# Moving the last weighted sum of the attention heads from the next step's first slot to the end of its own step

## The chip, the core and the metric

The kernel runs on one core of a Trainium2 chip. The metric is the device time of one execution in microseconds (us); the times given are medians of several runs. The core has five engines that run side by side and meet through semaphores: TensorE (PE in the profile, its weight loads PEld), VectorE (DVE), ScalarE (ACT), GpSimd (POOL) and SyncE (SP), which issues most of the DMAs.

## What is computed

One decoder layer over an input `x` of 32 x 256 x 256 (32 sequence positions, 256 tokens, 256 channels) with a context of the same shape:

```python
x = _layernorm(x + _L0_attn_ref(x, lmlg, theta, last_conv_init))      # long convolution: a complex
                                                                      # decay per channel, real part times x
x = _layernorm(x + _L0_xattn_ref(x, ctx, ctx, ...))                   # cross attention, 16 heads of 16
x = _layernorm(x + _L0_ffn_ref(x, scale, centroids, up_w, down_w))    # each token to one of 8 experts
```

Inside the cross attention, per position:

```python
Qp, Kp, Vp = relu(Q @ Wq + bq), relu(K @ Wk + bk), relu(V @ Wv + bv)
probs = softmax(einsum('bqhd,bkhd->bhqk', q, k) / dh ** 0.5)
out = einsum('bhqk,bkhd->bqhd', probs, v).reshape(B, T, C) + Qp       # then a layer norm
```

The change concerns the second `einsum`, the weighted sum of the values, for the last four of the 16 heads.

## The kernel before

The first part treats one sequence position (256 tokens) as one item, and runs a software pipeline over the 32 items. Each engine has its own instruction list, written out by a function `step(t)` that is called for t = -2 to 34. In one step an engine works on several items at once: `cur` = t gets its scores and their maxima, `prv` = t - 1 its transposed scores, exponentials and weighted sums, `n` = t + 1 its projections, `a` = t - 2 the end of its attention, `b` = t - 3 its routing to the experts, and t + 2 and t + 3 the convolution. The step is cut into 16 places, h = 0 to 15, one for each head. An engine executes its list strictly in the order written; a `wait` holds up all that is behind it on the same engine.

TensorE at each even h computes, for heads h and h + 1, the scores of `cur` (line 1004, to the banks `S`) and the transposed scores of `prv` (line 1017, to the banks `T`). The first scores of a step wait for the stacks of queries and keys, which go through DRAM: GpSimd makes the low pieces `q_lo` and `k_lo` (line 770), SyncE writes them out and reads them back. They wait also for VectorE's maxima of the step before, since there are two banks.

VectorE takes the maxima (line 1243). ScalarE takes the exponentials of `T` (line 864) into the ring `probs`, which holds eight heads. `weighted_sum(item, grp)` (lines 970 to 983) multiplies the probabilities of four heads with the values: 16 matmuls whose outputs are 32 columns each (line 980), into half of the bank `O`. It waits for the four exponentials (`exp_ok`) and for `O` to be free (`o_ev`), and signals `pv`. Groups 0, 1 and 2 run at h = 8, 10 and 13 of the item's step as `prv`. Group 3 runs in the next step, at h = 1, when the item has become `a`. ScalarE copies `O` to `oT` by `copy_sums` (line 854): pair 0 at h = 11, pair 1 in the next step at h = 2. At h = 4 and 5 of that step TensorE transposes `oT` (line 1069), and VectorE divides and adds (lines 1359, 1362, 1370).

Around the place left: at h = 0 TensorE transposes `x1` (line 960), at h = 1 the maxima (`neg_flip`, line 967), which ScalarE copies to `nm_row` in `neg_round` (line 832); SyncE's `write_neg` waits for that. At h = 2 and 3 follows the projection of the queries (line 988), at 6 and 7 that of the keys. Around the place entered: at h = 14 TensorE transposes `q32` (line 1130), at h = 15 the context `ct` for the item after next (line 960), and then comes the next step.

VectorE's order at the start of a step is: maxima 0 and 1, `row` of item `b` (line 1258, waits for GpSimd's `rs`, line 729), maxima 2 and 3, the product `u` (line 1266), maxima 4 and 5. GpSimd's product `by_re` (line 694) belongs to the convolution. `slot` (line 1425, at h = 12) is VectorE's last step of the routing, and releases GpSimd's scatter (line 802).

When all items are through, the second part takes 71 tiles of 128 tokens through their experts (lines 371 to 528). It is the same before and after.

Of the kernel before, what the change touches and what calls it, by code (L numbers as in the profile page):

```python
# [81 lines left out]
def build(nc, x, ctx_in, lmlg, theta, last_conv, Wq, bq, Wk, bk, Wv, bv, ln_g, ln_b, ffn_scale, centroids, up_w, down_w, out):  # L82
    stack = ExitStack()
    with stack:
# [145 lines left out]
        def wait(eng, name, item, per=1, j=None):  # L230

            if not item.runtime and item.k >= SEQ:
                item, j = Item(0, SEQ - 1), per
            wait_value(eng, name, item.times(per, per if j is None else j))
# [28 lines left out]
        def active(item):  # L263
            return item.within(0, SEQ)
# [271 lines left out]
        with nc.Block() as block:  # L536
# [276 lines left out]
            def _(act):  # L813
# [14 lines left out]
                def neg_round(item, half, b):  # L828

                    wait(act, "negT", item, 2, half + 1)  # L830
                    wait_value(act, "neg_out", item.times(32, 16 * half))
                    a_.activation(nm_row[:, :], M_ps[b][0:HPC, 0:TOK], ACT.Copy).then_inc(s["neg_ok"], 1)
# [16 lines left out]
                def copy_sums(item, pair):  # L849

                    wait(act, "pv", item, 4, 2 * pair + 2)
                    if pair == 0:
                        wait(act, "x_pe", item - 1, 2)
                    a_.activation(oT[:, 2 * pair:2 * pair + 2, :].rearrange("p g t -> p (g t)"), O_ps[:, :], ACT.Copy).then_inc(s["o_ev"], 1)
# [12 lines left out]
                def step(t):  # L867
                    prv, n, a, b = t - 1, t + 1, t - 2, t - 3
                    for h in range(H):
                        if h % 2 == 0:  # L870
                            exponentials(prv, h)
                            exponentials(prv, h + 1)
                        if h == 0:
                            if active(n):
                                wait(act, "x1T_pe", n)
                                wait(act, "q_pe", n - 1, 2)
                                a_.activation(x1T[:, :, :].rearrange("p o t -> p (o t)"), M_ps[0][:, :], ACT.Copy).then_inc(s["x1T_ok"], 1)  # L877
                        if h == 14 and active(n):
                            wait(act, "qn_pe", n)
                            wait(act, "oq_ok", n - 4, 2)  # L880
                            a_.activation(qn[:, n.mod(4)].rearrange("p c d -> p (c d)"), M_ps[2][:, :], ACT.Copy).then_inc(s["qn_ok"], 1)
                        if h == 15 and active(n + 1):
                            wait(act, "ctT_pe", n + 1)
                            wait(act, "v_pe", n, 2)
                            a_.activation(ctT[:, :, :].rearrange("p o t -> p (o t)"), M_ps[0][:, :], ACT.Copy).then_inc(s["ctT_ok"], 1)
                        if h == 1 and active(prv):
                            neg_round(prv, 1, 2)
                        if h == 9 and active(t):
                            neg_round(t, 0, 0)
                        if h == 2 and active(a):  # L890
                            copy_sums(a, 1)
                        if h == 3:
                            if active(n):

                                wait(act, "q_pe", n, 2)
                                wait(act, "qn_pe", n - 1)
                                wait_ring(act, q_out[(n - 1).mod(2)], n - 1, 2, 32)
                                for dst in (q_hi, q32):
                                    for c in range(NCH):
                                        a_.activation(dst[:, c], M_ps[0][:, c * TOK:(c + 1) * TOK], ACT.Relu,  # L900
                                                      bias=bq_sb[:, c:c + 1]).then_inc(s["q_ok"], 1)
                        if h == 7 and active(n):
                            wait(act, "k_pe", n, 2)
                            wait(act, "k_cut", n - 1)
                            wait_ring(act, k_out[(n - 1).mod(2)], n - 1, 2, 32)
                            for dst in (k_hi, k32):
                                for c in range(NCH):
                                    a_.activation(dst[:, c], M_ps[1][:, c * TOK:(c + 1) * TOK], ACT.Relu,
                                                  bias=bk_sb[:, c:c + 1]).then_inc(s["k_ok"], 1)
                        if h == 3 and active(b):  # L910
                            wait(act, "xnT_pe", b)
                            wait(act, "dist_pe", b - 1)
                            a_.activation(xnT[:, :, :].rearrange("p o t -> p (o t)"), M_ps[2][:, :], ACT.Copy).then_inc(s["xnT_ok"], 1)
                        if h == 13 and active(n):
                            wait(act, "v_pe", n, 2)
                            wait(act, "pv", n - 4, 4)
                            a_.activation(v_aug[:, n.mod(4), :, 0:H * VW].rearrange("p k (h w) -> p k h w", w=VW)[:, :, :, 0:DH],
                                          M_ps[1][:, :].rearrange("p (k h w) -> p k h w", k=NTC, w=DH), ACT.Relu).then_inc(s["v_ok"], 1)
                        if h == 4 and active(b):

                            wait(act, "xw_ok", b)
                            wait(act, "rms", b, 4)
                            wait(act, "offset", b - 1)
                            for c in range(NTC):
                                if c:
                                    wait(act, "nx_ok", b, 2, 1)
                                a_.activation(junk[:, :], xw[:, c], ACT.Square, scale=row[:, b.mod(2), c, C:C + 1],
                                              accum_out=nx[:, c:c + 1]).then_inc(s["nx_ok"], 1)
                        if h == 11 and active(prv):
                            copy_sums(prv, 0)  # L930
                        for e in HI_AT.get((t.k, h), ()):
                            upper(e)
# [5 lines left out]
            def _(pe):  # L938
# [17 lines left out]
                def flip(dst, src):  # L956

                    for oc in range(NCH):
                        for tc in range(NTC):
                            last = t_.transpose(dst[:, oc * TOK + tc * P:oc * TOK + (tc + 1) * P], src[:, tc, oc * P:(oc + 1) * P], ident[:, :])  # L960
                    return last
# [8 lines left out]
                def weighted_sum(item, grp):  # L970

                    wait(pe, "exp_ok", item, H, 4 * grp + 4)
                    if grp == 0:
                        wait(pe, "v_ok", item)

                    wait_value(pe, "o_ev", item.times(2, grp // 2))
                    for kc in range(NTC):
                        for j in range(4):
                            h = 4 * grp + j
                            last = t_.matmul(O_ps[32 * j:32 * j + 32, (grp % 2) * TOK:(grp % 2 + 1) * TOK],  # L980
                                             v_aug[:, item.mod(4), kc, h * VW:h * VW + 32], probs[:, h % 8, kc, :],
                                             start=(kc == 0), stop=(kc == NTC - 1))
                    last.then_inc(s["pv"], 1)
# [37 lines left out]
                def step(t):  # L1021
                    cur, prv, n, a, b = t, t - 1, t + 1, t - 2, t - 3
                    for h in range(H):
# [8 lines left out]
                        if h == 1:  # L1032
                            if active(prv):
                                wait(pe, "qn_ok", t)
                                neg_flip(prv, 1, 2)
                            if active(a):
                                weighted_sum(a, 3)
                        if h == 2 and n.k == 0:
                            pe.wait_ge(s["params"], PARAMS * 16)
                            pe.wait_ge(s["setup_pool"], 12)  # L1040
# [94 lines left out]
                        if h == 15 and active(n + 1):  # L1135
                            nn = n + 1
                            wait_ring(pe, ctx_in_s[nn.mod(2)], nn, 2, 16)
                            wait(pe, "neg_ok", cur, 2, 1)
                            if t.edge():
                                wait(pe, "q_ok", n, 4)  # L1140
                                wait(pe, "o_ok", a, 4)
                            flip(M_ps[0], ct[:, nn.mod(2)]).then_inc(s["ctT_pe"], 1)

                steps(pe, step)
                tensor2(pe)

# [313 lines left out]
```

## Time and profile before

| | |
|---|---|
| time, median of 3 runs | 1257.54 us (1252.96 to 1257.8) |
| profiled execution: time, span | 1257.0 us, 1255.2 us |
| mean granted TensorE clock | 0.935 |
| TensorE busy (matmuls) | 1119.9 us, 89% |
| VectorE busy | 942.7 us, 75% |
| GpSimd busy | 783.9 us, 62% |
| ScalarE busy | 669.9 us, 53% |
| weighted sums (line 980), 2048 matmuls | 151.0 us busy |
| maxima (line 1243), 512 | 328.3 us busy, 71.0 us idle before |

Times within a view count from the start of the span. Matmuls overlap, and their ends are modelled; so the distance from the start of one group to the start of the next says more about their cost than their busy time. A bracket behind an instruction gives how long its engine was idle before it, and what ended that. The granted clock is TensorE's: 1.00 is 2.4 GHz, 0.50 is 1.2 GHz.

### The profile page before, as it was taken

The page shows a single profiled execution, that of the slowest core. Times are in us where ns is not written, and L with a number is a line of the kernel's source. Part 1 is how long each engine was busy: PE and PEld are TensorE (multiplying, and loading weights), DVE is VectorE, ACT ScalarE, POOL GpSimd, SP SyncE. Part 2 cuts the span into 40 slices and gives each one's busy share as a digit, 9 for nine tenths or more (in the row PEclk, how much of TensorE's full clock was granted, in tenths as well). Part 3 has the DMA queues.
Part 4 walks back from the last instruction along what each step waited for, and adds up shares of the span by engine and source line. Part 5 has one row for each costly group of instructions (what it writes and reads, how often), then busy time and mean ns, then how long its engine had stood idle before and what let it go on. Part 6 is the DMA issues. An engine that isn't in the chain of part 4 may idle for free.

```text
span 1255.2 us, 27516 instructions
## 1 busy us (share of the span) xinstructions
PE 1119.9 (89%) x8060; PEld 820.0 (65%) x8061; DVE 942.7 (75%) x2416; ACT 669.9 (53%) x1416; POOL 783.9 (62%) x932
## 2 busy tenths in 40 slices
PE   3799989999999998989999999752999999999996
PEld 2466666666666666656666666431888888888885
DVE  7558998988988998999898898763555555555553
ACT  4166776766667776767676777641222222222221
POOL 4637888888878988879888865561233333333333
PEclk9689999999989999999999999555999999999998
DMA  4676676665555565556556555042111111111110
GB/s 131 146 179 194 174 207 183 182 156 139 141 140 146 149 158 137 147 139 161 136 146 156 136 134 126 11 151 59 44 51 47 43 50 50 49 47 48 50 51 22
DMA packets 90826, 144.91 MB, mean 115 GB/s; under 512 B 12663, under 2 KB 78336, under 8 KB 84513
## 3 DMA queue, kind: packets, MB, share of 16 engines
q1 hardware_dynamic: 83616, 126.09, 38.6%
q0 software_dynamic: 6528, 16.99, 4.6%
q8 instruction: 55, 0.90, 0.3%
q10 hardware_dynamic: 576, 0.53, 0.2%
q14 instruction: 51, 0.41, 0.1%
HBM read 91.44 MB, written 53.03 MB: 115 GB/s over the span
## 4 chain that ended last, share of the span: by engine, by line
PE 45%; DVE 19%; POOL 15%; issue 10%; DMA 8%; SPq 2%; ACT 1%; POOLq 0%; DVEq 0%; ACTq 0%
PE Y L454 10%; PE G L422 8%; PE A L422 8%; DVE neg_max_sb L1243 7%; PE S L1004 3%; PE M L988 3%; DMA k_st<-k_pieces 3%; DMA k_pieces<-k_lo 3%; DVE oq L1370 3%; POOL buckets L802 2%; PE GT L432 2%; PE O L980 2%; POOL rs L729 2%; POOL by_re L694 2%; PE M L960 2%
## 5 line engine op out<-in xcount | busy, mean ns | idle before, releaser
L1243 DVE TENSOR_REDUCE neg_max_sb<-S 128x2 f32<-128x512 f32 x512 | 328.3, 682 | 71.0 <-PE S L1004 69.2
L864 ACT ACTIVATE probs<-T 128x512 f32<-128x512 f32 x512 | 277.9, 595 | 148.1 <-PE T L1017 136.8
L1004 PE MATMUL S<-k_st,q_st 48*128 48x256 f32 x1024 | 215.3, 321 | 46.3 <-DMA k_st<-k_pieces 27.8
L1004 PEld LDWEIGHTS S<-k_st,q_st 48*128 48x128 f32 x1024 | 147.3, 194 | 123.7 <-issue 53.5
L1017 PE MATMUL T<-q_st,k_st 49*128 49x256 f32 x1024 | 211.9, 321 | 9.8 <-ACT probs L864 8.1
L1017 PEld LDWEIGHTS T<-q_st,k_st 49*128 49x128 f32 x1024 | 148.0, 195 | 28.3 <-ACT probs L864 17.0
L399 ACT ACTIVATE gT<-GT 128x512 f32<-128x512 f32 x71 | 42.5, 599 | 209.4 <-PE GT L432 209.4
L980 PE MATMUL O<-probs,v_aug 128*32 128x256 f32 x2048 | 151.0, 416 | 0.7 <-ACT probs L864 0.7
L378 POOL DMA_INDIRECT out<-res,token x71 | 76.4, 1077 | 103.3 <-DVE res L499 98.8
L454 PE MATMUL Y<-dn_sb,gT 128*128 x568 | 134.2, 379 | 0.8 <-ACT gT L399 0.8
L802 POOL DMA_INDIRECT buckets<-row,slot x64 | 69.7, 1089 | 85.0 <-DVE slot L1425 74.8
L454 PEld LDWEIGHTS Y<-dn_sb,gT 128*128 128x128 f32 x568 | 107.5, 189 | 18.3 <-issue 1.0
L422 PE MATMUL G<-up_hi,xsT 128*128 x284 | 107.7, 420 | 1.2 <-DVE xsT L504 1.0
L422 PE MATMUL A<-up_hi,xsT 128*128 x284 | 107.1, 418 | 0.0
L383 POOL TENSOR_SCALAR rs<-mv 128x1 f32<-128x1 f32 x71 | 16.0, 226 | 142.4 <-DVE mv L528 142.2
L499 DVE TENSOR_SCALAR res<-y,mv,rs 128x256 f32<-128x256 f32 x71 | 29.4, 414 | 86.1 <-POOL rs L385 86.1
L980 PEld LDWEIGHTS O<-probs,v_aug 128*32 128x32 f32 x2048 | 56.5, 115 | 56.2 <-ACT probs L864 16.0
L694 POOL TENSOR_TENSOR by_re<-state,decay 128x1024 f32<-128x1024 f32 x31 | 73.4, 2366 | 1.2 <-DVE x L1330 0.9
L403 ACT ACTIVATE gate<-G 128x512 f32<-128x512 f32 x71 | 42.4, 597 | 58.7 <-PE G L422 58.7
L988 PE MATMUL M<-ctT,wk_sb 128*128 128x256 f32 x256 | 67.0, 407 | 6.1 <-issue 6.0
L1116 PE MATMUL M<-wv_sb,ctT 128*128 128x256 f32 x256 | 70.5, 399 | 0.0
L988 PE MATMUL M<-x1T,wq_sb 128*128 128x256 f32 x256 | 68.2, 411 | 0.8 <-ACT x1T L877 0.8
(184 smaller groups left out, 2541.1 us busy)
## 6 DMA issues: line engine op xcount, KB each, us to landing
q_st<-q_pieces SPq DMA_DIRECT2D x64, 256.0 KB
k_st<-k_pieces SPq DMA_DIRECT2D x64, 256.0 KB
xr<-buckets SPq DMA_DIRECT2D x71, 129.0 KB, 2.1
xt<-in_x SPq DMA_DIRECT2D x32, 256.0 KB, 6.3
ct<-in_ctx SPq DMA_DIRECT2D x32, 256.0 KB, 6.8
q_pieces<-q_hi SPq DMA_DIRECT2D x32, 256.0 KB, 2.1
q_pieces<-q_lo SPq DMA_DIRECT2D x32, 256.0 KB, 2.2
q_st<-q_pieces SPq DMA_DIRECT2D x64, 128.0 KB
```

The costliest lines, as they stand in the source:

```text
L378: g.indirect_dma_start(out=out_rows, out_offset=bass.IndirectOffsetOnAxis(ap=token[:, f.mod(2):f.mod(2) + 1], axis=0), in_=res[:, f.mod(2) ...
L422: last = t_.matmul(ps[:, :], xT[:, w, c * P:(c + 1) * P], src[:, bass.ds(off + c * 2 * HID, HID)], start=(k == 0), stop=(k == len(terms) - 1))
L454: last = t_.matmul(Y_ps[:, 0:C], gT[:, m.mod(2), c * P:(c + 1) * P], dn_sb[:, bass.ds(off + c * C, C)], start=(c == 0), stop=(c == HCH - 1))
L694: g.tensor_tensor(by_re[:, :, :, :], state[:, 0].unsqueeze(1).to_broadcast(both), pair_b, ALU.mult).then_inc(s["conv"], 1)
L802: g.indirect_dma_start(out=buckets[:, :], out_offset=bass.IndirectOffsetOnAxis(ap=slot[:, p, c:c + 1], axis=0), in_=row[:, p, c, :], in_of ...
L864: a_.activation(probs[:, h % 8].rearrange("p k t -> p (k t)"), T_ps[h % 2][:, :], ACT.Exp, scale=DH ** -0.5).then_inc(s["exp_ok"], 1)
L980: last = t_.matmul(O_ps[32 * j:32 * j + 32, (grp % 2) * TOK:(grp % 2 + 1) * TOK], v_aug[:, item.mod(4), kc, h * VW:h * VW + 32], probs[:, ...
L988: last = t_.matmul(dst[:, oc * TOK:(oc + 1) * TOK], w[:, ic, oc * P:(oc + 1) * P], xT[:, ic, :], start=(ic == 0), stop=(ic == NCH - 1))
L1004: last = t_.matmul(S_ps[h % 2][:, c * TOK:(c + 1) * TOK], q_st[base:base + STACK, h, c * P:(c + 1) * P], k_st[base:base + STACK, h, :], st ...
L1017: last = t_.matmul(T_ps[h % 2][:, c * TOK:(c + 1) * TOK], k_st[base:base + AUG, h, c * P:(c + 1) * P], q_st[base:base + AUG, h, :], start= ...
L1116: last = t_.matmul(M_ps[1][:, c * C:(c + 1) * C], ctT[:, ic, c * P:(c + 1) * P], wv_sb[:, ic, :], start=False, stop=(c == NTC - 1 and ic = ...
L1243: v.tensor_reduce(neg_max[:, cur.mod(2), :, h], S_ps[h % 2][:, :].rearrange("p (c t) -> p c t", c=NTC), AX.X, ALU.max, negate=True).then_i ...
```

## The change

`weighted_sum(a, 3)` at h = 1 is removed from TensorE's step, and `weighted_sum(prv, 3)` is put at h = 15, behind the transposes of `ct`. It is the same item, one step earlier in the list. ScalarE's `copy_sums(a, 1)` moves within its step from h = 2 (behind exponentials 2 and 3 and behind `nm_row`) to h = 0, behind the copy of `x1T`.

```diff
@@ -875,6 +875,8 @@
                                 wait(act, "x1T_pe", n)
                                 wait(act, "q_pe", n - 1, 2)
                                 a_.activation(x1T[:, :, :].rearrange("p o t -> p (o t)"), M_ps[0][:, :], ACT.Copy).then_inc(s["x1T_ok"], 1)
+                            if active(a):
+                                copy_sums(a, 1)
                         if h == 14 and active(n):
                             wait(act, "qn_pe", n)
                             wait(act, "oq_ok", n - 4, 2)
@@ -887,8 +889,6 @@
                             neg_round(prv, 1, 2)
                         if h == 9 and active(t):
                             neg_round(t, 0, 0)
-                        if h == 2 and active(a):
-                            copy_sums(a, 1)
                         if h == 3:
                             if active(n):
 
@@ -1033,8 +1033,6 @@
                             if active(prv):
                                 wait(pe, "qn_ok", t)
                                 neg_flip(prv, 1, 2)
-                            if active(a):
-                                weighted_sum(a, 3)
                         if h == 2 and n.k == 0:
                             pe.wait_ge(s["params"], PARAMS * 16)
                             pe.wait_ge(s["setup_pool"], 12)
@@ -1140,6 +1138,8 @@
                                 wait(pe, "q_ok", n, 4)
                                 wait(pe, "o_ok", a, 4)
                             flip(M_ps[0], ct[:, nn.mod(2)]).then_inc(s["ctT_pe"], 1)
+                        if h == 15 and active(prv):
+                            weighted_sum(prv, 3)
 
                 steps(pe, step)
                 tensor2(pe)
```

## Rows read from the trace of the kernel before

**Rows 1.** the page: busy time of each engine, and granted TensorE clock in 40 slices.

```profile
PE 1119.9 (89%) x8060; PEld 820.0 (65%) x8061; DVE 942.7 (75%) x2416; ACT 669.9 (53%) x1416; POOL 783.9 (62%) x932
...
PEclk9689999999989999999999999555999999999998
```

**Rows 2.** windows, 17 full-clock slots: length, busy time of PE, PEld, DVE, ACT, POOL, clock.

```profile
396.60:419.53 22.93, 21.77 (x210) 14.88 (x198) 22.00 (x57) 17.14 (x38) 20.44 (x22) 1.00 0.58 147
...
514.08:538.16 24.08, 22.18 (x210) 14.97 (x198) 23.16 (x57) 17.21 (x38) 19.92 (x22) 1.00 0.63 152
...
sum 396.80, PE 369.21 PEld 253.17 DVE 378.28 ACT 287.34 POOL 335.33; mean PE 21.72 PEld 14.89 DVE 22.25 ACT 16.90 POOL 19.73
```

**Rows 3.** windows, nine slots with a clock drop, same columns.

```profile
489.30:514.08 24.78, 22.57 (x194) 15.63 (x190) 20.28 (x57) 16.50 (x37) 20.50 (x22) 0.93 0.59 145
...
sum 223.04, PE 206.38 PEld 140.18 DVE 185.09 ACT 149.16 POOL 183.77; mean PE 22.93 PEld 15.58 DVE 20.57 ACT 16.57 POOL 20.42
```

**Rows 4.** timeline of VectorE, full-clock slot: start, length, engine, line, idle before.

```profile
402.11 0.74 DVE L1258 TENSOR_SCALAR row<-oq,mv,rs 128x256 f32<-128x256 f32 x2 [0.60 <-POOL rs L729]
...
402.91 1.29 DVE L1243 TENSOR_REDUCE neg_max_sb<-S 128x2 f32<-128x512 f32 x2
404.12 2.52 DVE L1266 SCALAR_TENSOR_TENSOR u<-state,xt 128x512 f32<-128x512 f32 x1
...
412.17 1.28 DVE L1243 TENSOR_REDUCE neg_max_sb<-S 128x2 f32<-128x512 f32 x2
```

**Rows 5.** timeline of GpSimd in the same slot.

```profile
403.72 2.37 POOL L694 TENSOR_TENSOR by_re<-state,decay 128x1024 f32<-128x1024 f32 x1
```

**Rows 6.** timeline of VectorE in a slot with a drop.

```profile
498.34 1.29 DVE L1243 TENSOR_REDUCE neg_max_sb<-S 128x2 f32<-128x512 f32 x2 [2.30 <-PE S L1004]
499.55 1.01 DVE L1266 SCALAR_TENSOR_TENSOR u<-state,xt 128x512 f32<-128x512 f32 x1
```

**Rows 7.** waits between 111 and 757 us: total, times, longest.

```profile
DVE neg_max_sb L1243 <- PE S L1004: 38.0, 32, 2.5
```

**Rows 8.** timeline of TensorE around two step starts with a drop.

```profile
375.77 0.50 PE L1004 MATMUL S<-k_st,q_st 48*128 48x256 f32 x2 [1.10 <-DMA k_st<-k_pieces]
...
493.35 0.50 PE L1004 MATMUL S<-k_st,q_st 48*128 48x256 f32 x2 [2.12 <-DMA k_st<-k_pieces]
...
496.38 1.49 PE L980 MATMUL O<-probs,v_aug 128*32 128x256 f32 x16
```

**Rows 9.** timeline of TensorE, full-clock slot: step starts, and projection of keys.

```profile
399.66 0.38 PE L1004 MATMUL S<-k_st,q_st 48*128 48x256 f32 x1 [0.69 <-DMA k_st<-k_pieces]
...
400.57 0.66 PE L960 MATMUL M<-ident,x 128*128 128x128 f32 x4
401.06 0.38 PE L967 MATMUL M<-ident,neg_max_sb 128*8 128x128 f32 x2
401.38 1.07 PE L980 MATMUL O<-probs,v_aug 128*32 128x256 f32 x16
...
402.38 0.38 PE L1004 MATMUL S<-k_st,q_st 48*128 48x256 f32 x1
...
409.31 1.97 PE L988 MATMUL M<-ctT,wk_sb 128*128 128x256 f32 x8 [0.38 <-issue]
411.20 0.38 PE L1004 MATMUL S<-k_st,q_st 48*128 48x256 f32 x1
...
422.90 0.50 PE L1004 MATMUL S<-k_st,q_st 48*128 48x256 f32 x2 [1.43 <-DMA k_st<-k_pieces]
```

**Rows 10.** timeline of ScalarE in the same slot.

```profile
397.78 1.09 ACT L864 ACTIVATE probs<-T 128x512 f32<-128x512 f32 x2 [0.87 <-PE T L1017]
...
401.76 0.36 ACT L832 ACTIVATE nm_row<-M 8x256 fp32r<-8x256 f32 x1
...
403.93 0.60 ACT L854 ACTIVATE oT<-O 128x512 f32<-128x512 f32 x1
```

**Rows 11.** chain of work that ended last, at the next step's start: start, length, what.

```profile
425.00 1.00 PE O L980 x16
```

## The prediction

> **What bounds the kernel now.** I began with the page. Attention and routing fill the first 800 us or so; the expert tiles after them don't contain the edited lines, so the change must show in the first part. VectorE is busy for 75% of the whole span, and the row of the granted clock shows dips among its nines [rows 1]. I therefore cut the steady part into slots, from the end of one cast of `slot` (L1425) to the end of the next: one slot is one step of the pipeline. The view by windows puts them into two kinds. In 17 slots the clock stayed at its upper level; together they take 396.8 us, 23.34 us each, with VectorE busy for 22.25 us of it [rows 2]. In nine slots the granted clock dropped to half (1.2 of 2.4 GHz) for some microseconds; they take 223.0 us, 24.78 us each, and VectorE is busy for only 20.57 us [rows 3]. A slot with a clock drop is thus 1.44 us longer.
>
> The timelines say why. In a full-clock slot VectorE has one idle of note, 0.60 us before it writes `row` (L1258), which waits for GpSimd's `rs`; then come maxima 2 and 3, and then the product `u`, whose 2.52 us end half a microsecond after GpSimd's `by_re` product (403.72 + 2.37 = 406.09) [rows 4, 5]. In a half-clock slot the same `u` lasts 1.01 us, because it starts later [rows 6]. So in a full-clock slot VectorE is tied to GpSimd and not to TensorE: `u` holds up to about 1.5 us of waiting that absorbs a late TensorE. In the half-clock slot VectorE waits 2.30 us for the scores of head 2 [rows 6]. In the waits, all idle of the maxima behind scores comes to 38.0 us in the steady part [rows 7].
>
> Where do the drops come from? Before the first scores of a step TensorE stands idle, since the stack of keys is still in flight: 1.10 us (at 375.77) and 2.12 us (at 493.35) in two steps whose clock then fell, against 0.69 us (399.66) in one where it did not [rows 8, 9]. The long holes sit right behind the eight transposes that close the step.
>
> **The change part by part.** (1) *Sixteen matmuls leave the first slot of the next step.* They take 1.00 us there, from 401.38 to the scores at 402.38 [rows 9], and 1.49 us at 496.38, where the clock is low for part of them [rows 8]. Scores 2 and the projection of queries come that much sooner. In the full-clock slot this gives nothing: maxima 2 and 3 are queued behind `row`, which waits for GpSimd, and behind them `u` waits anyway [rows 4, 5]. Gain: 0 in 17 slots. The cover is the 0.60 us wait plus the slack in `u`.
>
> (2) *They enter at the end of their own step, behind the transposes of `ct`.* They need the last exponential. The two exponentials there begin at 397.78 and take 1.09 us, so they end at 398.87 [rows 10]. The sum then runs from about 398.95 to 399.95, and the first scores start 0.3 us later than 399.66 [rows 9]. That delay falls on maxima 0, which have little slack, but it eats half of the 0.60 us wait before `row` and is gone there [rows 4]. In steps with holes of 1.1 us or more it fits wholly inside the hole: cost 0. On TensorE the queue behind the new wait for `exp_ok` is the next step's first scores and all after them; it would cost if ScalarE fell behind by more than 1 us, and nothing shows that.
>
> (3) *The change of array shape.* The sum uses 32 columns of the array, its new neighbours on both sides use more; formerly the transposes of the maxima stood before it. What entering costs is seen in part: the four transposes at 400.57 take 0.49 us to the next start, thus 0.12 each; the two behind them take 0.32 us to the sum's start, which leaves at most 0.08 us for the entry [rows 9]. Bounds: 0 to 0.1 us per step, hidden in the hole; I take 0. The Trainium skill (TensorEngine Tiling (Array Packing), Key Properties) says that changing the tiling mode drains TensorE, which speaks against the move, as one more mode change per step is made. The page gives no price; by its rule a sum that counts 0.08 us for each of 32 steps would come out 2.6 us higher if nothing hid the drain.
>
> (4) *ScalarE's copy of the sums* (0.60 us) moves from behind exponentials 2 and 3 to right behind the copy of `x1T`, ahead of `nm_row` and those exponentials [rows 10]. `nm_row` and SyncE's `write_neg` behind it come about 0.5 us later, and so does everything that SyncE has behind that wait. The next entry of weight there waits for the query activations, which depend on the projection and come later than `nm_row` in any case. Exponentials 2 and 3 do not start until their scores are there, which is now earlier. Bounds: 0 to 0.5 us of lateness on a path with slack. I take 0.
>
> (5) *The clock.* The hole behind the transposes gets 1.0 us of matmuls. A hole of 1.10 to 2.12 us becomes one of 0.1 to 1.1 us [rows 8]. The drops follow holes of 1.1 us and more (not each such hole has one: 1.43 us at 422.90 has none [rows 9]), so most of them should go, and with them VectorE's 2.30 us wait. Nine slots would then cost 23.34 instead of 24.78 us: 9 x 1.44 = 13.0 us [rows 2, 3]. The bounds of this term: none if the drops remain; at the top 9 x (24.78 - 22.93) = 17 us, if all converted slots are of the shorter sort of full-clock slot. There are two sorts, 22.93 and 24.08 us, VectorE busy 22.00 and 23.16 us [rows 2]. It is the same work, so 1.16 us of it is a wait inside an instruction against GpSimd; which sort a slot becomes is a race that the change doesn't touch on purpose.
>
> (6) *TensorE's idle time moves.* In full-clock slots TensorE is not the bound, so the microsecond comes up again later: where the projection of keys waits behind VectorE's division. There TensorE idles 0.38 us now (before 409.31) [rows 9]; with 1.0 us less work and 0.3 us later start ahead of it, the hole becomes about 1.1 us. This is at the lower edge of the holes that preceded drops [rows 8]. I allow 1 to 2 us in the sum for a drop or two here.
>
> (7) *The ends.* The last steps get the same sum after the same exponential, with nothing between: 0 to 1 us.
>
> Sum: 0 (1 to 4) - 13.0 (5) + 1.5 (6) - 0.5 (7) = -12 us. The profiled execution took 1257.0 us for its span of 1255.2 us, and the median of the runs is 1257.5 us, so the two agree. Predicted: 1257 - 12 = 1245 us.
>
> **The rivals.** *A, the drop only moves.* The new hole of about 1.1 us before the projection of keys takes the place of the old one. A drop there adds as much again to the projection, 1.9 us (409.31 to 411.20) [rows 9]; scores 8 behind it are ready some 0.5 us before VectorE takes them at 412.17 [rows 4], so it costs about 1.3 us. If it occurs in as many slots as now, 9 to 10, the result is -12 + 12: 1257 us. For it: the size of the hole. Against it: a hole of 1.10 us is the smallest that I find ahead of a drop, and holes of 0.69 us and less go without one [rows 8, 9].
>
> *B, slower, by the same mechanism in most slots.* If all full-clock slots get the new hole, then all 26 can be hit. At 1.3 us each it decides from 14 hits on (18 us against 12 us gained, which leaves +6); at 20 hits the time is 1257 - 12 + 26 = 1271 us.
>
> *C, the drops don't go.* The hole may not be what drops the clock, or what is left of it may still do. Then the delay and the saving cancel behind `u`: -6 us if half of the drops remain, 1251 us; 1256 us if all do.
>
> *D, the sum is on the path as the chain shows it.* The chain that ended last runs through it at 425.00 with its 1.00 us [rows 11], and a reader of this view alone would expect 32 x 1.0 = 32 us and 1225 us. Against it: `row` and `u` wait for GpSimd right behind it, in 17 of 26 slots [rows 2, 4].
>
> *E, the shared memory port.* The Trainium skill (SBUF — State Buffer, section SBUF: two separate sides) calls the port pair that VectorE and GpSimd share an exclusive lock held for the whole instruction; by that, `u` ends when `by_re` lets go. As a mechanism of this kernel: were every slot of the longer sort, 26 slots of 24.08 us would take 626.1 us against 619.8 us now (396.8 + 223.0), which makes 1257 + 6 = 1263 us; were all of the shorter sort, 596.2 us and 1233 us [rows 2, 3]. The `u` of 2.52 and 1.01 us agrees with the lock [rows 4, 6].
>
> **How the numbers follow.** Forecast, drops mostly gone (1238 to 1251): 0.53. A, together with C at half or more and the mild side of E (1251 to 1263): 0.29. B and the bad end of E (over 1263): 0.12. D and the good end of E (under 1238): 0.06. A measurement of this kernel can tell about 0.5%, 6.3 us, from no change. Faster than 1251.2: 0.53 + 0.06, 0.59; within 0.5%: 0.29; slower than 1263.8: 0.12. The range takes in the short-sort end of E and all of A and C: 1234 to 1263 us.
>
> **What would show it.** Steady slots near 23.3 us with the granted clock at 1.00 in nearly all; the maxima's idle behind scores down from 38.0 us to under 15 us; the hole before a step's first scores down to 0 to 1.1 us, with the sum starting within 0.2 us of the last exponential's end; TensorE idle of about 1 us before the projection of keys; `u` near 2.5 us in nearly every slot. The prediction is wrong if slots at full clock are themselves shorter (D), if drops appear 8 us into a step (A, B), or if the clock falls as often at the step's start although the hole is filled (C).

## The result, and the profile after

The changed kernel is not faster. Over 20 runs of each, its median is 1258.2 us (1251.25 to 1267.91) against 1255.8 us (1245.2 to 1265.7); the ratio on record is 1.0051, 95% interval 1.0027 to 1.0076 (it is not the quotient of the two medians, which would be 1.0019). I had forecast 1245 us. In a second comparison on another occasion (after_again, below) the ratio was 0.9997 (0.9972 to 1.0022). So it is the same, or slower by half a percent; 1% faster it is not.

The profiled execution of the changed kernel is one of its slower ones (span 1263.7 us). Its page:

```profile
PE 1133.2 (90%) x8029; PEld 829.6 (66%) x8061; DVE 972.0 (77%) x2416; ACT 667.2 (53%) x1416; POOL 771.2 (61%) x932
...
PEclk9579999999999999998989999655999999999998
...
L1243 DVE TENSOR_REDUCE neg_max_sb<-S 128x2 f32<-128x512 f32 x512 | 327.0, 680 | 52.2 <-PE S L1004 52.1
...
L988 PE MATMUL M<-ctT,wk_sb 128*128 128x256 f32 x256 | 81.3, 474 | 22.3 <-issue 22.2
```

The first two lines answer to [rows 1]. VectorE idles less ahead of the maxima (52.2 us over the whole span, against 71.0 us in the table above). The last line is the projection of keys. In the page of the kernel before, the same group reads:

```profile
L988 PE MATMUL M<-ctT,wk_sb 128*128 128x256 f32 x256 | 67.0, 407 | 6.1 <-issue 6.0
```

TensorE now idles 22.3 us ahead of this projection instead of 6.1 us, and the projection itself takes 81.3 us instead of 67.0 us.

By windows, cut from one cast of `slot` to the next as before, 17 slots kept the full clock, and nine had a drop (length, busy time of PE, PEld, DVE, ACT and POOL, granted clock); this answers to [rows 2] and [rows 3]. The 17:

```profile
162.37:186.22 23.85, 22.04 (x201) 14.92 (x194) 22.69 (x57) 16.78 (x37) 19.71 (x22) 1.00 0.65 188
186.22:208.98 22.76, 21.46 (x197) 14.85 (x194) 21.76 (x58) 16.61 (x37) 20.26 (x22) 1.00 0.63 183
...
sum 401.11, PE 372.50 PEld 253.93 DVE 384.24 ACT 283.89 POOL 330.82; mean PE 21.91 PEld 14.94 DVE 22.60 ACT 16.70 POOL 19.46
```

And the nine:

```profile
519.33:543.71 24.38, 23.16 (x205) 15.84 (x194) 22.45 (x58) 16.74 (x38) 19.96 (x22) 0.93 0.55 138
567.42:593.12 25.70, 24.41 (x201) 16.49 (x194) 23.13 (x58) 16.67 (x37) 19.58 (x22) 0.87 0.54 136
...
sum 225.89, PE 212.55 PEld 144.17 DVE 207.21 ACT 150.66 POOL 178.04; mean PE 23.62 PEld 16.02 DVE 23.02 ACT 16.74 POOL 19.78
```

The drops are as many as before, nine, and a slot with one is 25.10 us (225.89 / 9) against 23.59 us without. Only their place has changed. All nine now begin 11.9 to 13.6 us behind the cast of `slot`; in the kernel before they began 3.7 to 5.6 us behind it.

TensorE's timeline of a full-clock slot (start, length, engine, line, shapes; idle before in brackets) shows the new order, and answers to [rows 9]:

```profile
378.31 0.60 PE L960 MATMUL M<-ident,ct 128*128 128x128 f32 x4
378.86 1.07 PE L980 MATMUL O<-probs,v_aug 128*32 128x256 f32 x16
...
380.93 0.66 PE L960 MATMUL M<-ident,x 128*128 128x128 f32 x4
381.42 0.38 PE L967 MATMUL M<-ident,neg_max_sb 128*8 128x128 f32 x2
...
389.68 0.67 PE L988 MATMUL M<-ctT,wk_sb 128*128 128x256 f32 x2 [0.91 <-issue]
```

The sum fills the hole: in this slot there is no idle in front of the first scores. The hole in front of the projection of keys has grown from 0.38 us to 0.91 us. In a slot with drops the projection behind it looks like this, and VectorE's maxima 8 pay:

```profile
580.15 3.75 PE L988 MATMUL M<-ctT,wk_sb 128*128 128x256 f32 x8 [0.91 <-issue]
583.83 0.58 PE L1004 MATMUL S<-k_st,q_st 48*128 48x256 f32 x1
```

```profile
584.66 1.29 DVE L1243 TENSOR_REDUCE neg_max_sb<-S 128x2 f32<-128x512 f32 x2 [1.57 <-PE S L1004]
...
585.94 1.39 DVE L1370 TENSOR_TENSOR oq<-o,qn 128x256 f32<-128x256 f32 x1
587.26 1.25 DVE L1405 TENSOR_TENSOR onehot_bf<-expert_no,choice 128x16 bf16<-128x16 f32 x1
```

The projection takes 3.75 us at half the clock (1.2 GHz) against 1.97 us in [rows 9], and VectorE waits 1.57 us for the scores behind it. The last line of the second fence is the other thing of note. `onehot_bf` is 128x16, and takes 0.16 to 0.2 us when nothing is in its way; here it takes 1.25 us. In this profile it did so in 19 of 26 slots, in the first profile of the kernel before in 8 of 26. That is the difference of the two sorts of full-clock slots, some 23.9 and 22.8 us. In every long case the instruction ends 0.03 us behind the end of a product of GpSimd that was under way, `k_lo` or, in the slots where `k_lo` came earlier, `state`.

Two of the forecast signs came true without the time. Over the stretch of [rows 7] the maxima's idle behind scores fell from 38.0 to 14.1 us. And `u` (line 1266) now takes some 2.6 us in nearly every slot, where it took 1.01 us in the slot with a drop of [rows 6]:

```profile
DVE neg_max_sb L1243 <- PE S L1004: 14.1, 15, 1.6
...
L1266 DVE SCALAR_TENSOR_TENSOR u<-state,xt x26: 1426/2604/2632, 144.2 to 749.4; 128x512 f32<-128x512 f32 x26
```

So a part of what VectorE no longer waits for scores it now spends inside `u`. The three durations are the shortest, the median and the longest, in ns.

### The profile page after: what moved, and what is told of

It is laid out like the page before. It is cut to its first block, busy times and chain, and to the rows that moved or that the text cites. A ratio compares the mean times of both kernels' runs of the same rounds, so it can differ in the third digit from the quotient of the medians.

```text
span 1263.7 us, 27485 instructions
## 1 busy us (share of the span) xinstructions
PE 1133.2 (90%) x8029; PEld 829.6 (66%) x8061; DVE 972.0 (77%) x2416; ACT 667.2 (53%) x1416; POOL 771.2 (61%) x932
## 4 chain that ended last, share of the span: by engine, by line
PE 41%; DVE 28%; issue 12%; POOL 10%; DMA 6%; SPq 1%; ACT 1%; POOLq 0%; DVEq 0%; ACTq 0%
DVE neg_max_sb L1243 12%; PE Y L454 10%; PE G L422 8%; PE A L422 8%; PE M L988 4%; DVE oq L1370 3%; POOL buckets L802 3%; PE S L1004 3%; PE GT L432 2%; POOL state L720 2%; DVE u L1266 2%; DMA k_pieces<-k_lo 2%; DVE onehot_bf L1405 2%; POOL rs L729 2%; DMA k_st<-k_pieces 2%
## 5 line engine op out<-in xcount | busy, mean ns | idle before, releaser
L1243 DVE TENSOR_REDUCE neg_max_sb<-S 128x2 f32<-128x512 f32 x512 | 327.0, 680 | 52.2 <-PE S L1004 52.1
L1004 PE MATMUL S<-k_st,q_st 48*128 48x256 f32 x1024 | 224.4, 325 | 24.0 <-DMA k_st<-k_pieces 11.6
L1017 PE MATMUL T<-q_st,k_st 49*128 49x256 f32 x1024 | 219.3, 323 | 5.2 <-ACT probs L864 3.5
L1004 PEld LDWEIGHTS S<-k_st,q_st 48*128 48x128 f32 x1024 | 150.0, 195 | 111.0 <-issue 46.1
L1017 PEld LDWEIGHTS T<-q_st,k_st 49*128 49x128 f32 x1024 | 148.7, 194 | 22.3 <-ACT probs L864 16.0
L980 PE MATMUL O<-probs,v_aug 128*32 128x256 f32 x2048 | 144.1, 401 | 2.5 <-ACT probs L864 2.5
L988 PE MATMUL M<-ctT,wk_sb 128*128 128x256 f32 x256 | 81.3, 474 | 22.3 <-issue 22.2
L988 PEld LDWEIGHTS M<-ctT,wk_sb 128*128 128x128 f32 x256 | 58.1, 238 | 37.2 <-issue 27.6
```

Source lines behind the costliest of these rows:

```text
L988: last = t_.matmul(dst[:, oc * TOK:(oc + 1) * TOK], w[:, ic, oc * P:(oc + 1) * P], xT[:, ic, :], start=(ic == 0), stop=(ic == NCH - 1))
L1004: last = t_.matmul(S_ps[h % 2][:, c * TOK:(c + 1) * TOK], q_st[base:base + STACK, h, c * P:(c + 1) * P], k_st[base:base + STACK, h, :], st ...
L1017: last = t_.matmul(T_ps[h % 2][:, c * TOK:(c + 1) * TOK], k_st[base:base + AUG, h, c * P:(c + 1) * P], q_st[base:base + AUG, h, :], start= ...
L1243: v.tensor_reduce(neg_max[:, cur.mod(2), :, h], S_ps[h % 2][:, :].rearrange("p (c t) -> p c t", c=NTC), AX.X, ALU.max, negate=True).then_i ...
```

## The experiments

Three theories stood at the start. *Theory 1*: the hole on TensorE in front of a burst is what lets the clock fall; the change moves the hole, and the drops with it. *Theory 2*: the change tips the race of `onehot_bf` against GpSimd's `k_lo`, and that takes back the gain. *Theory 3*: the drops cost nothing, as other waits take their place.

### The two kernels again

No edit in either.

> The kernel before once more, unchanged, as the measure of chance. Both theories: ratio 1.00 within about 0.5%. Theory 1 (the clock drop sits in the hole ahead of the step's first scores): 6 to 12 steady slots with a drop, all of them 4 to 6 us behind the cast of slot. Theory 2 (the onehot instruction against GpSimd's k_lo is a race that the change tips): 7 to 12 of 26 onehot instructions at 1.26 us, as in the first profile (9); theory 2b (the race is chance from one execution to the next): anything from 5 to 20.

> The changed kernel once more, unchanged. Theory 1: no drop at 4 to 6 us behind the cast of slot, 6 to 12 drops at 12 to 14 us, where TensorE now idles ahead of the projection of keys. Theory 2: 17 to 22 of 26 onehot instructions at 1.26 us, as in the first profile of this kernel; theory 2b: anything from 5 to 20, and then the slower slots of the first profile were in part chance. Ratio to the kernel before 1.003 to 1.007.

Measured: before_again 1256.6 us, ratio 1.0013 (0.9983 to 1.0044), 14 slots with a drop (all at 3.7 to 5.8 us), 11 long onehots. after_again 1257.0 us, ratio 0.9997 (0.9972 to 1.0022), 12 slots with a drop, 11 of them at 12.0 to 13.7 us, and 13 long onehots. So the place of the drops belongs to the kernel, and their number and that of the long onehots vary from one execution to the next (8 and 11, 19 and 13). Theory 2 in its first form falls: as far as these profiles show, the race is chance.

### Filling the new hole with work that is moved

```diff
-                        if h == 8 and active(prv):
+                        if h == 6 and active(prv):
                             weighted_sum(prv, 0)
```

> The changed kernel, and weighted sum 0 moved from h = 8 to h = 6, ahead of the projection of keys, so that 1.0 us of real work lies in the hole there. If that hole is the cause of the drops (theory 1), drops at 12 to 14 us fall from nine to two or fewer, and the time falls by 9 x 1.5 = 13 us, ratio about 0.994 to the kernel before. If the drops have another cause (TensorE needs less time in all, and the clock falls wherever it idles), they turn up at the next hole, behind the projection, and the ratio stays at 1.00 to 1.01.

Measured: 1253.8 us, ratio 0.9948 (0.9915 to 0.9982). The drops at 12 to 14 us are gone, and 20 of 26 slots have one at 17.5 to 19.4 us instead, near the next place where TensorE is ahead of VectorE. Two of its slots, with a drop and without:

```profile
373.79:397.36 23.57, 22.57 (x193) 15.39 (x190) 21.86 (x58) 16.34 (x38) 20.18 (x22) 0.93 0.58 149
```

```profile
420.96:445.03 24.07, 22.29 (x209) 15.05 (x202) 23.15 (x58) 17.26 (x38) 19.90 (x22) 1.00 0.61 147
...
sum 142.48, PE 132.53 PEld 89.79 DVE 135.44 ACT 101.66 POOL 111.80; mean PE 22.09 PEld 14.97 DVE 22.57 ACT 16.94 POOL 18.63
```

The sum is that of the six slots without a drop. At this place a drop costs little: the 20 slots take 23.92 us on average, the six 23.75 us. Compared within a sort, the 13 slots with a drop and a long `onehot_bf` take 23.94 us, the five with a long `onehot_bf` alone 23.92 us; with a short `onehot_bf` the slots with a drop take 23.6 us (but for the first, 25.7 us), against 22.7 to 23.0 us at full clock in the changed kernel. So the drop is free in one sort and costs some 0.7 us in the other. The holes ahead of these drops are short, nearly all of some 0.6 us; in the slot at 373.79:

```profile
390.13 0.50 PE L1004 MATMUL S<-k_st,q_st 48*128 48x256 f32 x2 [0.63 <-DVE neg_max_sb L1243]
```

So the second answer of the expectation was right for the drops (they move on), and the first nearly for the time. Theory 1 holds for the place, and a drop's price depends on what stands behind it.

### Filling the holes with work that is added

If a spare microsecond of TensorE wanders from hole to hole, it should vanish when work is added and none taken away. In before_dup a sum is computed twice, with the same inputs to the same place:

```diff
-                def weighted_sum(item, grp):
+                def weighted_sum(item, grp, again=False):
...
-                    last.then_inc(s["pv"], 1)
+                    if not again:
+                        last.then_inc(s["pv"], 1)
...
                             flip(M_ps[0], ct[:, nn.mod(2)]).then_inc(s["ctT_pe"], 1)
+                        if h == 15 and active(prv):
+                            weighted_sum(prv, 2, again=True)
```

> The kernel before, with weighted sum 2 computed a second time at h = 15, behind the transposes of ct (same inputs, same output, no signal): 1.0 us of matmuls in the hole ahead of the first scores, and nothing taken away elsewhere. Theory 1 (the hole drops the clock): no drop at 4 to 6 us behind the cast of slot, and none at 12 to 14 us either, since TensorE has no time to spare there; 9 to 14 slots become 1.4 to 2 us shorter, ratio 0.985 to 0.99. Theory 3 (the drop costs nothing, other waits take its place): same drops gone, ratio 1.00.

Measured: 1243.7 us, ratio 0.9878 (0.9836 to 0.9919), one slot with a drop among 27. The sum of its 26 full-clock slots, by windows:

```profile
133.59:157.69 24.10, 22.88 (x222) 15.25 (x214) 23.05 (x57) 17.02 (x38) 19.84 (x22) 1.00 0.75 198
...
sum 603.05, PE 584.32 PEld 396.02 DVE 569.90 ACT 434.53 POOL 508.24; mean PE 22.47 PEld 15.23 DVE 21.92 ACT 16.71 POOL 19.55
```

That is 23.19 us a slot, 0.15 us less than the full-clock slots of the kernel before (23.34 us). TensorE does a microsecond more per step, and the kernel is 15 us faster. Theory 3 falls. The same in the changed kernel, with the second computing in the new hole:

```diff
+                        if h == 6 and active(prv):
+                            weighted_sum(prv, 0, again=True)
                         if h == 8 and active(prv):
                             weighted_sum(prv, 0)
```

> The changed kernel, with weighted sum 0 computed twice, at h = 6 ahead of the projection of keys without a signal and again at its place at h = 8. TensorE has as much work in a step as in the run before_dup, with the filling in both holes. Theory 1: drops at 12 to 14 us gone (9 and 12 in the two profiles of the changed kernel), none new, ratio 0.985 to 0.99. Theory 1b (less work per step, not the place of the hole, is what lets the clock fall): the same, as the work is back. If drops turn up at 17 to 18 us as in after_fill, the freed time has moved on although nothing was taken away.

Measured: 1245.7 us, ratio 0.9896 (0.9858 to 0.9934), two slots with a drop among 27, none of them at 12 to 14 us. As in before_dup, no slice of the page's clock lies below 9 in the steady part:

```profile
PEclk9689999999999999999999998755999999999998
```

To find whether a smaller filling is enough, before_half computes two of the four heads again:

```diff
-                        for j in range(4):
+                        for j in range(2 if again else 4):
```

> As before_dup, but the second computing of sum 2 covers two of its four heads: 8 matmuls instead of 16. Theory 1 (what is left of the hole decides): the holes of 1.1 to 2.1 us become 0.4 to 1.6 us, so the longest still have a drop behind them: 1 to 5 drops at the step's start instead of 9 to 14, ratio 0.989 to 0.996. If any matmul at that place is enough: no drops, ratio 0.988 as in before_dup. If eight do nothing: ratio 1.00.

Measured: 1244.0 us, ratio 0.9884 (0.983 to 0.9939), one slot with a drop among 27. It does not tell the sizes apart, since half of the matmuls fill the same time:

```profile
322.93 1.06 PE L980 MATMUL O<-probs,v_aug 128*32 128x256 f32 x8
324.09 0.35 PE L1005 MATMUL S<-k_st,q_st 48*128 48x256 f32 x1
```

Nor does it close every hole. One of those left is longer than the shortest that preceded a drop at this place in the kernel before (1.10 us), and it had no drop; the one drop that is left followed a hole of 1.56 us:

```profile
696.92 0.50 PE L1005 MATMUL S<-k_st,q_st 48*128 48x256 f32 x2 [1.33 <-DMA k_st<-k_pieces]
```

And before_dup2 has both fillings, that of before_dup and that of after_dup:

> As before_dup, with sum 0 also computed a second time at h = 6, ahead of the projection of keys: 2 us of idle work per step. Theory 1: no drop at all is left (one in before_dup), but the projection starts some 0.5 us later, which is about the slack of VectorE's maxima 8: ratio 0.985 to 0.992, no better than before_dup. If TensorE had been near the bound after all, every step grows by 0.5 to 1 us: ratio 1.00 or more.

Measured: 1259.0 us, ratio 0.9985 (0.9954 to 1.0016), with one slot with a drop among 26. Its 25 full-clock slots take 23.75 us on average. The drops are gone, yet the time is back. Twenty of the 25 slots take 22.8 to 24.1 us, as in the other kernels; five take 24.4 to 25.7 us, and in each of them VectorE waits for scores three to five times. Two neighbours:

```profile
327.77:353.26 25.49, 24.28 (x242) 16.01 (x234) 22.47 (x57) 17.19 (x38) 19.80 (x22) 1.00 0.62 153
353.26:376.21 22.95, 22.77 (x226) 15.39 (x222) 21.88 (x57) 16.30 (x37) 20.45 (x22) 1.00 0.53 139
```

So with two microseconds of added work TensorE is late for VectorE in some steps. The profile is that of the slowest of 12 executions (1266.8 us), so how much of the median this explains stays open. The run bounds the remedy from above: one microsecond is to be had for nothing, the second costs all that the clock gives.

### The parts of the change alone

pe_only is the changed kernel with this undone:

```diff
-                            if active(a):
-                                copy_sums(a, 1)
...
+                        if h == 2 and active(a):
+                            copy_sums(a, 1)
```

> The changed kernel with ScalarE's copy of the sums back at h = 2; only TensorE's part of the change is left. If the copy's place is of no account, as forecast: drops at 12 to 14 us as in the changed kernel, ratio 1.00 within 0.4%. If the copy ahead of exponentials 2 and 3 is what makes the projection of keys wait, the drops are fewer, ratio 0.995 or less.

Measured: 1259.2 us, ratio 0.9994 (0.9964 to 1.0025); 12 slots with a drop, ten of them at 11.9 to 13.3 us. Six onehots are long. TensorE's part by itself makes the picture of the changed kernel.

act_only has ScalarE's part, and the sum at h = 1 as before:

> ScalarE's part of the change alone: the copy of the sums at h = 0, while TensorE still computes sum 3 at h = 1. The copy then waits for the sum and holds up nm_row and exponentials 2 and 3 behind it by about 1 us. If that has slack, as forecast for half a microsecond: drops at the step's start as in the kernel before, ratio 1.00 within 0.5%. If not: 1.005 to 1.03.

Measured: 1259.2 us, ratio 1.0008 (0.9968 to 1.0047); 11 slots with a drop, all at 3.7 to 6.3 us, ten long onehots. The copy in its new place waits 0.49 us for the sum, and no cost of it can be measured:

```profile
571.96 0.60 ACT L877 ACTIVATE x1T<-M 128x512 f32<-128x512 f32 x1
573.05 0.60 ACT L854 ACTIVATE oT<-O 128x512 f32<-128x512 f32 x1 [0.49 <-PE O L980]
573.55 0.36 ACT L832 ACTIVATE nm_row<-M 8x256 fp32r<-8x256 f32 x1
```

### The onehot

In after_port the instruction with two inputs from memory is replaced by two with a scalar per partition:

```diff
-                        v.tensor_tensor(onehot_bf[:, :, :], expert_no[:, :, :], ch, ALU.is_equal).then_inc(s["pick"], 1)
+                        for c in range(NTC):
+                            last = v.tensor_scalar(onehot_bf[:, c], expert_no[:, c], choice[:, c:c + 1], None, ALU.is_equal)
+                        last.then_inc(s["pick"], 1)
```

> The changed kernel, with the onehot made by two tensor_scalar instructions (the choice as a scalar per partition) in place of one tensor_tensor with two inputs from memory. If the 1.26 us of the tensor_tensor is a wait for the memory port that GpSimd's k_lo holds (theory 2), both instructions take 0.1 to 0.2 us each in every slot, and each of the 19 long slots is 1.0 us shorter: 15 to 19 us, ratio about 0.99. If the wait only moves on to the next instruction of VectorE, or GpSimd loses what VectorE gains, the ratio stays at 1.00 to 1.01 although the onehot is short.

Measured: 1292.4 us, ratio 1.0295 (1.0262 to 1.0328). Both answers of the expectation were wrong. VectorE's timeline, and then GpSimd's, in one slot:

```profile
530.68 1.71 DVE L1370 TENSOR_TENSOR oq<-o,qn 128x256 f32<-128x256 f32 x1
532.31 1.40 DVE L1406 TENSOR_SCALAR onehot_bf<-expert_no,choice 128x8 bf16<-128x8 f32 x2
```

```profile
530.61 1.28 POOL L770 TENSOR_TENSOR k_lo<-k,k_hi 128x512 fp32r<-128x512 f32 x1 [0.61 <-ACT k L908]
531.84 1.70 POOL L713 TENSOR_TENSOR state<-state,by_re 128x512 f32<-128x512 f32 x1
```

`oq` ends half a microsecond behind `k_lo` (532.39 and 531.89), the pair of tensor_scalar 0.2 us behind the next product of GpSimd (533.71 and 533.54). The two together take 1.4 us (12 slots) or 2.5 us (13 slots) in 25 of 26 slots, where the tensor_tensor got through in 0.2 us or less in 7 and in 13 of 26 slots of the changed kernel. In the slots of 2.5 us the pair outlasts `k_lo` and the product behind it. So this form is held up with GpSimd's products too, and in more slots. The six full-clock slots take 25.10 us, against 23.59 us and 23.36 us (327.1 / 14, after_again): what VectorE loses at this place shows in the length of the slot. This is compatible with the section on the two sides of the memory in the Trainium skill (SBUF — State Buffer, section SBUF: two separate sides), which names VectorE's 2-port modes as well as its instructions with two inputs; the runs show that this tensor_scalar ends with GpSimd's products, not which mode it is in.

## Why the prediction was wrong

**What bounds the kernel** was read rightly. Full-clock slots of the changed kernel take 23.59 and 23.36 us, against 23.34 us [rows 2]; with a long `onehot_bf` alone they take 23.9 us, against 24.0 us before. Taking a microsecond off the start of TensorE's step makes no such slot shorter, and rival D falls.

**Steps 1 to 4** hold. The delay of the first scores is swallowed, and in act_only the copy costs nothing that can be measured (1.0008). For the change of array shape the trace of after has the four transposes of `ct` at 378.31 and the sum at 378.86, 0.55 us later, where four of 0.12 us would end at 0.49 us: at most 0.06 us, inside the bound of 0.08 us. The last exponential ends at 378.81, so the sum may have waited for that and not for the array:

```profile
377.72 1.09 ACT L864 ACTIVATE probs<-T 128x512 f32<-128x512 f32 x2 [0.88 <-PE T L1017]
```

The full-clock slots show no loss from the change of shape.

**Step 5** was right in what the drops at that place cost. The drops at the step's start went, and where nothing took their place (before_dup) the gain was 1.2%, 15 us, against the 13.0 us of the sum. The reading that gave it was the cut of the steady part into slots by one instruction of the saturated engine, sorted by the granted clock.

**Step 6** failed. It found the right place and nearly the right size (a hole of "about 1.1 us", measured 0.91 us), and then allowed 1 to 2 us for "a drop or two". There were nine and eleven drops, at 25.10 - 23.59 = 1.5 us each: 14 us, which is all of the gain. I held the hole for too small, since the smallest that I had found in front of a drop was 1.10 us. But the length of one hole doesn't decide: 0.91 us had a drop at 580.15 and none at 389.68, and in after_fill 0.63 us had one. The trace of the kernel before could have told me. Beside the 1.43 us of [rows 9], six more of its 17 full-clock slots have a hole of 1.08 or 1.09 us at the step's start and no drop, two of them these:

```profile
158.02 0.35 PE L1004 MATMUL S<-k_st,q_st 48*128 48x256 f32 x1 [1.08 <-DVE neg_max_sb L1243]
...
181.87 0.35 PE L1004 MATMUL S<-k_st,q_st 48*128 48x256 f32 x1 [1.09 <-DVE neg_max_sb L1243]
```

Nor does a drop begin at a fixed distance from its hole: 1.7 to 3.5 us behind the hole's start in the kernel before, but in seven of the nine slots of the changed kernel within 0.8 us of it, while TensorE still stood idle. Rival A had the price (1.3 us) and the result (1257 us) nearly right, and its chance of 0.29, shared with others, was too low.

A stronger argument follows from step 1 itself. The change takes no work out of a step, it only moves it. If a full-clock slot does not get shorter, TensorE's idle time in it must stay what it was. The views show this: slot less TensorE's busy time is 23.34 - 21.72 = 1.62 us in the kernel before [rows 2], 23.59 - 21.91 = 1.68 us after, and 23.75 - 22.09 = 1.66 us in after_fill. Only the added work lowers it: 23.19 - 22.47 = 0.72 us in before_dup. The first three had drops in 9, 9 and 20 of 26 slots, the last in one of 27. after_fill gained its half percent not by fewer drops but by a place where they cost little. Whether the drops go with the single hole or with the idle time of the whole step, these runs don't separate, since every filling that removed them lowered both; the hole of 1.33 us that had no drop in before_half speaks against its length alone.

**Step 7 and E.** The range within E (which sort a slot becomes) is as wide as forecast: 8 to 19 long onehots of 26 in four profiles of the two kernels, at 1.1 to 1.2 us each, some 12 us. It is one of three reasons why single executions of one kernel differ by up to 20 us. The number of drops is another: of the 23 executions of the kernel before that stand beside before_half, the five fastest (1251.2 to 1255.2 us) had a mean granted clock of 0.939, the five slowest (1265.3 to 1269.9 us) of 0.930; over all 23 the correlation of time and clock is -0.78. The third lies ahead of the steady part. The first profile of after spans 9.2 us more than that of after_again, but the 26 slots take 627.0 and 625.3 us; 7.3 us of the difference have arisen when the first of them begins (136.7 and 129.4 us), with a lower clock in the pipeline's first steps, in after and then in after_again:

```profile
30.00:80.00 50.00, 39.73 (x143) 28.97 (x143) 25.75 (x49) 15.17 (x31) 24.85 (x22) 0.60 0.62 154
```

```profile
30.00:80.00 50.00, 36.92 (x160) 25.66 (x159) 27.32 (x45) 16.68 (x35) 27.21 (x23) 0.69 0.66 160
```

So the 19 long onehots did not make that execution slow by themselves; it had three drops fewer.

What stays open is whether the 0.5% of the first comparison is real. Its interval excludes 1, that of after_again does not, and pe_only's doesn't either. Nothing in the traces asks for more than zero.

## What to carry to other kernels

On an engine that is not the bound, moved work comes back as idle time at another wait, and here the granted clock fell at that wait too, so that the idle time cost something: follow the hole, count the slots it can hit, and price the drop at each. If full-clock stretches are bound by another engine, adding about a microsecond of repeated matmuls to the hole was worth 1.2% here (1243.7 us), and moving real work into it nothing (half a percent where a second move brought the drops to a cheaper place); a second microsecond took it all back. And before a mean over slots is trusted, look whether the slots are of two sorts by a race.

## What the runs showed of the hardware

Transposes right ahead of a hole didn't prevent the drop behind it (nine and 14 of 26 slots in the kernel before). The clock fell with holes of some 0.6 us (after_fill, a drop in 20 of 26 slots), 0.91 us and 1.10 to 2.12 us, and stayed up with others of 0.91, 1.09, 1.33 and 1.43 us. Half of a weighted sum put into the hole, eight matmuls over 1.06 us, left one drop in 27 slots. A matmul group of 32-column outputs takes the same time with two of its four column groups as with four (8 matmuls 1.06 us, 16 matmuls 1.07 us). A tensor_scalar on 128x8 elements with a bf16 output can be held up with GpSimd's products for as long as a tensor_tensor with two inputs (1.4 or 2.5 us for the pair, 1.25 us for the tensor_tensor). And at one instruction of VectorE against one of GpSimd the outcome differs from step to step: 0.16 or 1.25 us, in 6 to 19 of 26 slots the longer.
